# Neighbourhood attention and expert layer on one core: key and query loads in the order of use, the second image's load moved, one mask table

## The chip, the cores and the metric

One core of one Trainium2 chip. The time is the device time of one execution in microseconds (us), all loads and stores included. The engines are TensorE (PE), VectorE (DVE), ScalarE (ACT), GpSimd (POOL) and SyncE (SP). SP computes nothing here: it issues transfers. 16 DMA engines move the data.

## The reference, cut to what matters

Two images of 48 x 48 positions with 384 channels. Twice, the input is group-normalised, goes through a layer and is added to itself. The first layer is attention with 12 heads of width 32, where each position sees a 7 x 7 neighbourhood (moved inwards at the borders) and 16 registers:

```python
qkv = x @ qkv_w.T + qkv_b
scores = jnp.where(mask_cat[None, None], scores * scale, NEG_INF)
attn = jax.nn.softmax(scores, axis=-1)
o = jnp.einsum('bnqk,bnke->bnqe', attn, v_cat)
x = x + (o @ out_w.T + out_b)
```

The second layer is a mixture of four experts of which each position uses the best two. The change doesn't touch it.

## The kernel before, in words

The attention runs in six stages (`gi`, 0 to 5): two images times three groups of four heads. An image is cut in two ways. A *block* `a` (0 to 5) is 8 image rows; a *strip* `s` (0 to 5) is 8 image columns over all 48 rows. Keys are projected by blocks, everything else goes by strips.

A stage goes like this, and all its parts are written out by hand in the order in which each engine runs them; engines meet at semaphores, and each engine, SP and POOL too, goes through its list strictly in order.

1. PE projects the keys of the six blocks. ACT rounds each to fp16 (`KU`), DVE takes the rest (L523) and then copies both halves, opened out into windows, to `KT` (L531); `k_lo` counts the blocks for which both are done. SP writes `KT` to DRAM (`kscr`, L246).
2. PE projects the queries strip by strip (`queries`), between them the output projection of the stage before (`project_out`); POOL writes the queries to DRAM (`qscr`, L358).
3. SP brings keys and queries back in the layout of a strip: `KB` (four slots, three transfers a strip, L254) and `QS` (three transfers a strip, L260). For strips 0, 1, 4 and 5 it first loads 8 mask rows of the slot again (L251), as border strips have other column masks.
4. PE runs the scores that give each query's maximum (`scores`, L1184) in turns with the value projection (`values`). POOL writes the values to DRAM (`vscr`, L365), three transfers a strip, and SP brings them back as windows (`VR`, two buffers, six transfers a strip, L271).
5. PE, ACT and DVE go through the strips: `key_scores` (L1210) gives exponents' inputs, ACT takes the exponential (L890), `weighted` (L1233) sums values and weights. Between them stand the maximum scores of strips 3, 4 and 5. The maxima reach row 120 and 121 of `QS` by POOL's small transfers (L381).

In a stage SP's list is: 12 writes of keys; keys and queries of strips 0, 1, 2, 3; queries of 4 and 5; values of 0 and 1 (which wait until the values of both neighbouring strips have landed in DRAM); then keys of 4 (they wait until strip 0's slot is free), values of 2, keys of 5, values of 3, 4, 5.

The second image is loaded by POOL in stage 0, one sixth (576 KB) in each strip's pass, between its additions of the bias to `X` (L394). Stage 1 reads it first, in the pass of strip 0 (statistics on DVE).

PE waits touched by the change: the query projection of strips 0 and 1 waits for `k_lo` of blocks 2 and 3, since it writes the PSUM banks from which these were read; the first output projection waits for `k_lo` of all six blocks.

Of the kernel before, what the change touches and what calls it, by code (L numbers as in the profile page):

```python
# [17 lines left out]
STRIPS = H // 8  # L18
SN = H * CT_
KW = CT_ + WIN - 1  # L20
X0 = [CT_ * s - 3 for s in range(TILES)]
PADW = W + WIN - 1
CHUNK = P
LEAD, TAIL = 3 * KW + REGS, 3 * KW
# [25 lines left out]
def build(nc, x, wqkv, wo, fc1, fc2, rw, cst, fb2, qtab, ktab, gdown, gup, ident16, tri, pick, out):  # L50
    ctx = ExitStack()
    with ctx:
# [118 lines left out]
        def dve_lows(n, blk):  # L171
# [1 line left out]

        names = """c_in g_in i_in wo_in t_in whi wlo wohi wolo rhi rlo b16 zeros vpad bvhi bvlo bv_mm obx pads ones kr_mm kr_hi kr_lo vr_mm vr_sb krg
            gn_st gn_gs gn_gc gn_mm gn_var gn_sd gn_par gn_hi gn_t gn_ta gn_lo_p gn_lo_v ob_add
            k_mm k_hi k_lo q_mm q_hi q_lo v_mm v_sb o_mm op_done s_mm mx mxh t_mm t_ev st_mm exd pv sumt rinv norm os_hi os_lo
            vreg_in chain f_in fhi flo b2_in b2z b2s moe_in lg_mm ex_in ex_out comb csz ct_mm ct_sb
            h_mm cb_mm ge hf hh hl y_mm y_done y_out""".split()
        s_ = {n: sem(n) for n in names}
# [10 lines left out]
        def kb_count(gi, s):  # L190
            if s in (2, 3):
                return 48 * (gi + 1)
            return 128 * gi + (64 if s < 2 else 128)

        K_BANK = (4, 6, 2, 3, 5, 7)
        V_BANK = lambda gi, s: 7 if gi and s == TILES - 1 else 2 + s % 2
# [32 lines left out]
        def _(sp):  # L229
# [4 lines left out]
            sp.dma_start(raw_g[0], wqkv[:, 0, :]).then_inc(w_in[0], 16)  # L234
            sp.dma_start(QS[96:120, :, :], qtab.unsqueeze(1).broadcast_to([24, HEADS, N])).then_inc(s_["t_in"], 16)
            for i in range(4):
                sp.dma_start(KB[96:TROWS, :, i, :], ktab[1].unsqueeze(1).broadcast_to([26, HEADS, SLOTW])).then_inc(s_["t_in"], 16)
            for g in (1, 2):
                sp.dma_start(raw_g[g], wqkv[:, g, :]).then_inc(w_in[g], 16)
            sp.dma_start(raw_o, wo).then_inc(s_["wo_in"], 16)  # L240
# [5 lines left out]
                    sp.dma_start(kscr[part, :, :, a, :], KT[:, a % 3, part, :, :]).then_inc(kw_out[a % 3], 16)  # L246

            def keys_in(gi, s):
                if s in (0, 1, 4, 5):
                    kind = {0: 0, 1: 1, 4: 1, 5: 2}[s]  # L250
                    sp.dma_start(KB[112:120, :, slot(s), :], ktab[kind, 16:24].unsqueeze(1).broadcast_to([8, HEADS, SLOTW])  # L251
                                 ).then_inc(kb_in[slot(s)], 16)
                for j, part in enumerate((0, 1, 0)):
                    sp.dma_start(KB[DH * j:DH * (j + 1), :, slot(s), LEAD:LEAD + STRIPS * CHUNK],  # L254
                                 kscr[part, :, s, :, :].rearrange("(h d) a n -> d h (a n)", d=DH)).then_inc(kb_in[slot(s)], 16)
# [17 lines left out]
            for gi in range(STAGES):  # L273
                for a in range(STRIPS):
                    keys_out(gi, a)
                for i in range(3):
                    sp.wait_ge(kw_out[i], 64 * gi + 64)
                if gi == 0:
                    sp.wait_ge(s_["t_in"], 16 * 5)
                if 36 * gi > 0:  # L280
                    sp.wait_ge(s_["st_mm"], 36 * gi)
                for s in range(4):
                    keys_in(gi, s)
                    queries_in(gi, s)
                for s in (4, 5):
                    queries_in(gi, s)
                for s in (0, 1):
                    values_in(gi, s)
                for s in range(4):
                    if gi == 4 and s == 2:  # L290
                        for i in (2, 3, 4):
                            sp.wait_ge(v_out[i], 48 * (gi + 1))
                        sp.dma_start(wr_flat, fc1).then_inc(s_["f_in"], 16)
                    if s < 2:
                        sp.wait_ge(s_["st_mm"], 36 * gi + 6 * (s + 1))
                        keys_in(gi, s + 4)
                    values_in(gi, s + 2)
                    if gi == STAGES - 1 and s == 1:
                        for i in (0, 5):
                            sp.wait_ge(v_out[i], 48 * STAGES)  # L300
                        for src, dst in ((fc2, f2raw), (rw, rwraw)):
                            sp.dma_start(dst, src).then_inc(s_["f_in"], 16)
                        for j in range(3):
                            sp.dma_start(b2raw[DH * j:DH * j + EXPERTS, :], fb2).then_inc(s_["b2_in"], 16)
                        sp.dma_start(PICK[0:96, :], pick).then_inc(s_["moe_in"], 16)
# [15 lines left out]
        def _(pool):  # L321
# [75 lines left out]
            for gi in range(STAGES):  # L397
                register_keys(gi)
                for s in range(TILES):
                    queries_out(gi, s)  # L400
                if gi:
                    register_values(gi)
                for s in range(TILES):
                    values_out(gi, s)
                    if gi == 0 and s == 1:
                        register_values(gi)
                    if s in ((3, 4) if gi == 0 else (2, 4)):
                        maxima_in(gi, s // 2 - 1 if gi else s - 3)
                n = {2: 1, 5: 2}.get(gi)
                for s in range(TILES):  # L410
                    for a in range(STRIPS):
                        if a == 1 and s == 0:
                            maxima_in(gi, 2)
                        if a == 5 and s in (1, 2, 3):
                            maxima_in(gi, s + 2)
                        if a == 5 and s:
                            low_output(gi, s - 1)
                        if n and a % 2 == 1:
                            k = a // 2
                            if k in POOL_K[n]:  # L420
                                low_half(n, s, k)
                        if gi in (0, 3) and a % 2 == 0:
                            add_bias(gi // KC, a // 2, s)
                        if gi == 0 and a == 3:
                            c, at = s // 2, s % 2 * 3 * SN
                            pool.dma_start(xs(1, c, at, 3 * SN), x[1, :, c, at:at + 3 * SN]).then_inc(x_in[1][c][s % 2], 16)
                low_output(gi, TILES - 1)

            def hidden_low(m):
# [14 lines left out]
        def _(dve):  # L444
# [75 lines left out]
            def keys_low(gi, a):  # L520
                g = gi % KC
                dve.wait_ge(s_["k_hi"], 6 * gi + a + 1)
                link(V.scalar_tensor_tensor(out=KU[:, a % 2, 1, :, 3:3 + W], in0=ps[:, K_BANK[a], 0:SN].rearrange("p (r c) -> p r c", c=W),  # L523
                                            scalar=cols["qkb16"][:, KC + g:KC + g + 1], in1=KU[:, a % 2, 0, :, 3:3 + W],
                                            op0=ALU.add, op1=ALU.subtract))
                if 64 * gi + 32 * (a // 3) > 0:
                    dve.wait_ge(kw_out[a % 3], 64 * gi + 32 * (a // 3))
                if gi == 0 and a == 0:
                    dve.wait_ge(s_["pads"], 2)
                for part in range(2):  # L530
                    last = V.tensor_copy(KT[:, a % 3, part, :, 0:8 * KW].rearrange("p s (r c) -> p s r c", c=KW), windows(a, part))  # L531
                last.then_inc(s_["k_lo"], 1)
# [531 lines left out]
        def _(pe):  # L1064
# [53 lines left out]

            def queries(gi, s):
                if s < 2:  # L1120
                    pe.wait_ge(s_["k_lo"], 6 * gi + 3 + s)
                else:
                    pe.wait_ge(s_["q_lo"], 6 * gi + s - 1)
                split_product(ps[:, Q_BANK(s), 0:SN], lambda a, k: WQ[:, gi % KC, a, k, 0:P], lambda b, k: xh1(b, k, s * SN, SN)
                              ).then_inc(s_["q_mm"], 1)

            def project_out(gi, s):
                if s == 0:
                    pe.wait_ge(s_["k_lo"], 6 * gi + 12)
                    pe.wait_ge(s_["wolo"], 1)  # L1130
                pe.wait_ge(s_["os_lo"], 6 * gi + s + 1)
                if s == TILES - 1:
# [4 lines left out]
                    if gi in (1, 4):  # L1137
                        pe.wait_ge(s_["gn_par"], (gi + 1) // KC + 2)
                for j in range(KC):
                    if 0 < s < TILES - 1:  # L1140
                        pe.wait_ge(s_["op_done"], 18 * gi + KC * (s - 1) + j + 1)
                    split_product(ps[:, OP_BANK(gi, s, j), 0:SN], lambda a, k: WO[:, a, gi % KC, j * P:(j + 1) * P],
                                  lambda b, k: OS[:, b, s * SN:(s + 1) * SN], steps=1).then_inc(s_["o_mm"], 1)
# [299 lines left out]
def query_table():  # L1443
    import numpy as np
    out = np.zeros((24, TILES, H, CT_), np.float16)
    for r in range(H):
        out[r % 16, :, r, :] = BIG
    for c in range(CT_):
        out[16 + c, :, :, c] = BIG
    return out.reshape(24, N)  # L1450


def key_tables():
    import numpy as np
    out = np.zeros((3, 26, SLOTW), np.float16)
    out[:, 0:24, :] = -BIG
    out[:, 24:26, :] = MSCALE
    first = lambda q, size: min(max(q - WIN // 2, 0), size - WIN)
    for a in range(STRIPS):
        at = LEAD + CHUNK * a  # L1460
        for q in range(max(0, 8 * a - 8), min(H, 8 * a + 16)):
            for r in range(8):
                if first(q, H) <= 8 * a + r < first(q, H) + WIN:
                    out[:, q % 16, at + KW * r:at + KW * (r + 1)] = 0
            if q // 8 == a:
                out[:, q % 16, at + 8 * KW:at + CHUNK] = 0
        for kind, s in enumerate((0, 2, TILES - 1)):
            for c in range(CT_):
                f = first(CT_ * s + c, W)
                for i in range(KW):  # L1470
                    if f <= X0[s] + i < f + WIN:
                        out[kind, 16 + c, at + i:at + 8 * KW:KW] = 0
                out[kind, 16 + c, at + 8 * KW:at + CHUNK] = 0
    return out


# [49 lines left out]
```

## Time and profile before

| | |
|---|---|
| median of 3 runs | 649.22 us (649.11 to 655.11) |
| the profiled execution | 652.61 us, its span 650.8 us |
| PE busy (matmuls) | 567.0 us, 87% of the span |
| DVE, ACT, POOL busy | 455.8, 307.4, 282.7 us |
| DMA packets | 95.44 MB, 147 GB/s over the span |

The profiled execution is 1.81 us longer than its span, and 3.4 us above the median. Busy times are of one engine each and overlap. Stage 0 ends at about 107 us, stage 5 at about 505 us; the rest is the expert layer.

### The profile page before, as it was taken

What the parts mean: (1) busy time and instruction counts of PE and PEld (TensorE: products, weight loads), DVE (VectorE), ACT (ScalarE), POOL (GpSimd) and SP (SyncE); (2) the same over time, 40 slices, a digit from 0 to 9 for tenths busy, and PEclk for the clock granted to TensorE, in tenths of its full rate; (3) what the DMA queues carried; (4) which work ended last, traced back from release to release, by engine and by line L of the source; (5) the groups of instructions that cost most, each with busy time, mean ns of one, the idle gap of its engine ahead of it and who ended that gap; (6) DMA issues with size and microseconds to landing.
All of it is one profiled execution on the core that took longest, in us unless ns stands there. A gap on an engine that the chain in (4) does not pass through costs nothing.

```text
span 650.8 us, 22416 instructions
## 1 busy us (share of the span) xinstructions
PE 567.0 (87%) x9227; PEld 396.7 (61%) x9227; DVE 455.8 (70%) x1021; ACT 307.4 (47%) x609; POOL 282.7 (43%) x421
## 2 busy tenths in 40 slices
PE   3578879998899978998899987897987889998998
PEld 2346666677655756657675766655765546665554
DVE  6885575777887689676667767886689886863333
ACT  1762555215633288513563244541578337754221
POOL 3116798254222654436993362223744332413131
PEclk9999999999999999999999999999989999999999
DMA  9869774995339952398527966189551002121213
GB/s 305 188 148 287 201 217 119 230 275 156 98 89 220 256 144 71 87 255 227 154 57 177 260 177 165 35 201 256 170 145 48 2 0 74 38 74 37 74 37 109
DMA packets 131597, 95.44 MB, mean 147 GB/s; under 512 B 67324, under 2 KB 125352, under 8 KB 131496
## 3 DMA queue, kind: packets, MB, share of 16 engines
q1 hardware_dynamic: 121992, 75.18, 44.8%
q0 software_dynamic: 9504, 18.84, 9.3%
q8 instruction: 73, 1.20, 0.8%
q14 instruction: 28, 0.23, 0.1%
HBM read 57.62 MB, written 35.54 MB: 143 GB/s over the span
## 4 chain that ended last, share of the span: by engine, by line
PE 53%; DVE 16%; DMA 9%; SPq 7%; ACT 6%; issue 6%; POOL 2%; ACTq 0%; POOLq 0%; DVEq 0%
PE ps L1070 38%; SPq L271 5%; PE ps L1233 5%; PE ps L1184 4%; DVE MX L561 3%; DMA vscr<-VT 3%; DMA KB<-kscr 3%; PE ps L1210 3%; DVE ST L454 2%; ACT XH L831 2%; ACT PT L890 1%; DVE GT_ L493 1%; DVE SUMT L574 1%; DVE KT L531 1%; DMA kscr<-KT 1%
## 5 line engine op out<-in xcount | busy, mean ns | idle before, releaser
L561 DVE TENSOR_REDUCE MX<-ps 128x2 f32<-128x372 f32 x216 | 108.3, 541 | 63.9 <-PE ps L1184 62.9
L1070 PE MATMUL ps<-XH,WQ 128*128 128x384 f16 x810 | 140.6, 327 | 8.7 <-DVE XH L503 7.8
L1070 PEld LDWEIGHTS ps<-XH,WQ 128*128 128x128 f16 x810 | 77.6, 98 | 62.6 <-ACT XH L831 7.5
L890 ACT ACTIVATE PT<-ps 128x448 f32<-128x448 f32 (+1 forms) x162 | 78.7, 511 | 52.0 <-PE ps L1210 51.6
L1184 PE MATMUL ps<-KB,QS 120*32 120x186 f16 x1728 | 57.8, 250 | 27.0 <-DVE MX L561 10.6
L434 POOL TENSOR_TENSOR KT<-QS,KT 128x384 f16<-128x384 f32 x36 | 34.3, 962 | 95.3 <-ACT KT L983 95.3
L1210 PE MATMUL ps<-QS,KB 122*128 122x112 f16 (+1 forms) x864 | 64.3, 213 | 12.1 <-ACT PT L890 7.7
L1070 PE MATMUL ps<-WQ,XH 128*128 128x128 f16 x972 | 62.4, 222 | 5.2 <-issue 4.9
L381 POOL DMA_DIRECT2D QS<-MT x72 | 37.8, 529 | 59.5 <-ACT MT L880 59.1
L1210 PEld LDWEIGHTS ps<-QS,KB 122*128 122x128 f16 x864 | 43.3, 99 | 33.1 <-ACT PT L890 16.6
L1070 PEld LDWEIGHTS ps<-WQ,XH 128*128 128x128 f16 x972 | 56.0, 99 | 11.2 <-issue 8.8
L1233 PE MATMUL ps<-PT,VR 128*32 128x112 f32 (+1 forms) x1296 | 60.1, 258 | 2.5 <-DMA VR<-vscr 2.5
L1233 PE MATMUL ps<-PT,ONE 128*32 128x112 f32 (+1 forms) x1296 | 59.5, 254 | 0.8 <-issue 0.8
L1070 PE MATMUL ps<-OS,WO 128*128 128x384 f16 x324 | 57.6, 326 | 2.5 <-DVE X L545 1.5
L1070 PE MATMUL ps<-KT,WQ 128*128 128x384 f16 x324 | 58.6, 326 | 0.8 <-DVE X L726 0.5
L1184 PEld LDWEIGHTS ps<-KB,QS 120*32 120x32 f16 x1728 | 31.5, 97 | 43.5 <-DVE MX L561 16.8
L386 POOL TENSOR_TENSOR OS<-ON,OS 128x384 f16<-128x384 f32 x36 | 33.2, 922 | 33.2 <-ACT OS L896 32.9
L719 DVE TENSOR_TENSOR QS<-ps,QS 128x384 f32<-128x384 f32 x36 | 19.7, 555 | 39.1 <-POOL KT L434 14.1
L1070 PEld LDWEIGHTS ps<-OS,WO 128*128 128x128 f16 x324 | 31.0, 98 | 25.0 <-issue 3.0
L1070 PEld LDWEIGHTS ps<-KT,WQ 128*128 128x128 f16 x324 | 30.9, 98 | 23.8 <-DVE X L726 3.4
L394 POOL TENSOR_SCALAR X<-X,SM 128x384 f32<-128x384 f32 x36 | 44.4, 1242 | 0.4
L358 POOL DMA_DIRECT2D qscr<-QT x18 | 13.3, 741 | 71.2 <-DVE QT L537 71.1
(168 smaller groups left out, 1003.3 us busy)
## 6 DMA issues: line engine op xcount, KB each, us to landing
KB<-kscr SPq DMA_DIRECT2D x108, 192.0 KB, 7.0
kscr<-KT SPq DMA_DIRECT2D x72, 192.0 KB, 2.5
VR<-vscr SPq DMA_DIRECT2D x216, 56.0 KB
QS<-qscr SPq DMA_DIRECT2D x108, 96.0 KB, 6.6
out<-X SPq DMA_DIRECT2D x11, 576.0 KB, 3.3
X<-in_x SPq DMA_DIRECT2D x6, 576.0 KB, 7.3
qscr<-QT POOLq DMA_DIRECT2D x18, 192.0 KB, 3.3
qscr<-PT POOLq DMA_DIRECT2D x18, 192.0 KB, 5.3
```

Of the source, the lines that this page charges most:

```text
L271: sp.dma_start(VR[0:8 * KW, s % 2, a, :], vscr[8 * a:8 * a + 8, CT_ * s:CT_ * s + KW, :]).then_inc(vr_in[s % 2][a // 3], 16)
L381: pool.dma_start(QS[SROWS + part:SROWS + part + 1, :, s * SN:(s + 1) * SN], MT[part * HEADS:(part + 1) * HEADS, s % 2, :]).then_inc(m_in[s ...
L386: nc.gpsimd.tensor_tensor(OS[:, 1, s * SN:(s + 1) * SN], ON[:, s % 2, :], OS[:, 0, s * SN:(s + 1) * SN], ALU.subtract).then_inc(s_["os_lo" ...
L394: nc.gpsimd.tensor_scalar(xs(img, c, s * SN, SN), xs(img, c, s * SN, SN), cols["obx"][:, c:c + 1], None, ALU.add).then_inc(s_["ob_add"], 1)
L434: nc.gpsimd.tensor_tensor(HW[:, m % 2, 1, k, :], HF[:, unit % 2, :], HW[:, m % 2, 0, k, :], ALU.subtract).then_inc(s_["hl"], 1)
L561: V.tensor_reduce(out=MX[:, s % 2, t, 2 * pair:2 * pair + 2], in_=ps[:, S_BANK(s, i), 0:2 * RUN].rearrange("p (h n) -> p h n", h=2), op=AL ...
L719: V.tensor_tensor(HF[:, unit % 2, :], ps[:, 2 + k, 0:SN], GE[:, unit % 2, :], ALU.mult).then_inc(s_["hf"], 1)
L890: A(PTS[n % 4][:, 0:w], ps[:, ST_BANK(n), 0:w], ACT.Exp, scale=SCORE).then_inc(s_["exd"], 1)
L1070: last = mm(bank, lhsT(a, k), rhs(b, k), start=(k == 0 and n == 0), stop=(finish and k == steps - 1 and n == 2))
L1184: last = mm(ps[32 * j:32 * j + 32, S_BANK(s, i), hh * RUN:(hh + 1) * RUN], QS[0:SROWS, h, q0:q0 + 32], KB[0:SROWS, h, slot(s), at:at + RUN ...
L1210: last = mm(ps[:, ST_BANK(n), h * w:(h + 1) * w], KB[0:TROWS, h, slot(s), LEAD + CHUNK * a:LEAD + CHUNK * (a + 1)], QS[0:TROWS, h, s * SN ...
L1233: last = mm(ps[DH * h:DH * (h + 1), bank, CT_ * q0:CT_ * q1], lhsT, PTS[n % 4][:, h * w:(h + 1) * w], start=(a == 0), stop=(a == STRIPS - ...
```

## The change

- SP loads keys and queries of strips 0, 1 and 2, then waits until the six score units of strip 0 are done (`s_mm`), loads strip 3's keys and queries, then values of strips 0 and 1, and only then the queries of strips 4 and 5.
- The mask of all strips comes from one key table; the border strips' difference is put in the query table. The four mask loads of a stage go.
- The second image's six loads go from the six strip passes of stage 0 to the last three, two in each.
- A new semaphore `k_ps` counts the blocks whose PSUM bank DVE has read (L523), before the copies to `KT`. The query projections of strips 0 and 1 wait for it, and the first output projection waits bank by bank (blocks 1, 4, 5 of the next stage) in place of `k_lo`.

```diff
             def keys_in(gi, s):
-                if s in (0, 1, 4, 5):
-                    kind = {0: 0, 1: 1, 4: 1, 5: 2}[s]
-                    sp.dma_start(KB[112:120, :, slot(s), :], ktab[kind, 16:24].unsqueeze(1).broadcast_to([8, HEADS, SLOTW])
-                                 ).then_inc(kb_in[slot(s)], 16)
                 for j, part in enumerate((0, 1, 0)):
...
-                for s in range(4):
+                for s in range(3):
                     keys_in(gi, s)
                     queries_in(gi, s)
+                sp.wait_ge(s_["s_mm"], 36 * gi + 6)
+                keys_in(gi, 3)
+                queries_in(gi, 3)
+                for s in (0, 1):
+                    values_in(gi, s)
                 for s in (4, 5):
                     queries_in(gi, s)
-                for s in (0, 1):
-                    values_in(gi, s)
...
-                        if gi == 0 and a == 3:
-                            c, at = s // 2, s % 2 * 3 * SN
-                            pool.dma_start(xs(1, c, at, 3 * SN), x[1, :, c, at:at + 3 * SN]).then_inc(x_in[1][c][s % 2], 16)
+                        if gi == 0 and s > 2 and a in (1, 4):
+                            c, half = s - 3, a // 4
+                            at = half * 3 * SN
+                            pool.dma_start(xs(1, c, at, 3 * SN), x[1, :, c, at:at + 3 * SN]).then_inc(x_in[1][c][half], 16)
...
-                link(V.scalar_tensor_tensor(out=KU[:, a % 2, 1, :, 3:3 + W], in0=ps[:, K_BANK[a], 0:SN].rearrange("p (r c) -> p r c", c=W),
+                V.scalar_tensor_tensor(out=KU[:, a % 2, 1, :, 3:3 + W], in0=ps[:, K_BANK[a], 0:SN].rearrange("p (r c) -> p r c", c=W),
...
+                                       op0=ALU.add, op1=ALU.subtract).then_inc(s_["k_ps"], 1)
+                dve.wait_ge(s_["k_ps"], 6 * gi + a + 1)
...
                 if s < 2:
-                    pe.wait_ge(s_["k_lo"], 6 * gi + 3 + s)
+                    pe.wait_ge(s_["k_ps"], 6 * gi + 3 + s)
...
                 if s == 0:
-                    pe.wait_ge(s_["k_lo"], 6 * gi + 12)
...
-                    if 0 < s < TILES - 1:
+                    if s == 0:
+                        pe.wait_ge(s_["k_ps"], 6 * gi + (8, 11, 12)[j])
+                    elif s < TILES - 1:
```

## Rows read from the trace of the kernel before

**Rows 1.** Whom PE waited for, whole span: us in total, times, longest

```profile
PE ps L1184 <- issue: 6.9, 6, 3.4
PE ps L1184 <- DMA KB<-kscr: 6.7, 6, 1.7
PE ps L1070 <- issue: 4.9, 4, 1.9
...
PE ps L1233 <- DMA VR<-vscr: 3.1, 4, 1.6
...
PE ps L1070 <- DVE KT L531: 1.0, 2, 0.7
```

**Rows 2.** Timeline of SP in stage 4: start, us, issues merged by line

```profile
366.73 1.59 SPq L254 DMA_DIRECT2D KB<-kscr  x3
368.37 4.71 SPq L260 DMA_DIRECT2D QS<-qscr  x9
379.95 8.41 SPq L271 DMA_DIRECT2D VR<-vscr  x12
388.40 0.49 SPq L251 DMA_DIRECT2D KB<-in_ktab  x1
388.93 2.15 SPq L254 DMA_DIRECT2D KB<-kscr  x3
391.20 4.13 SPq L271 DMA_DIRECT2D VR<-vscr  x6
...
395.90 1.26 SPq L254 DMA_DIRECT2D KB<-kscr  x3
```

**Rows 3.** The chain of waits in stage 4: start, us, what

```profile
372.80 1.18 POOL vscr L365 x3
...
374.36 5.53 DMA vscr<-VT
...
390.65 3.17 DMA KB<-kscr
...
396.73 4.25 DMA KB<-kscr
```

**Rows 4.** DMA queues from 371 to 376 us: packets, MB, share of 16 engines

```profile
q1 hardware_dynamic: 1196, 1.10, 104.4%
q0 software_dynamic: 24, 0.03, 2.9%
```

**Rows 5.** Busy time by stretch, stage 4; last three: PEclk, DMA share, GB/s

```profile
380.00:384.00 4.00, 3.00 (x59) 2.26 (x58) 3.07 (x9) 2.51 (x7) 4.00 (x9) 1.00 0.44 126
```

**Rows 6.** Timeline of PE in stage 4: start, us, work [idle before it, until whom]

```profile
368.72 0.66 PE L1184 MATMUL ps<-KB,QS 120*32 120x186 f16 x24
...
393.86 0.50 PE L1184 MATMUL ps<-KB,QS 120*32 120x186 f16 x16 [1.65 <-DMA KB<-kscr]
...
401.03 0.50 PE L1184 MATMUL ps<-KB,QS 120*32 120x186 f16 x16 [1.15 <-DMA KB<-kscr]
```

**Rows 7.** Timeline of PE in stage 5

```profile
454.71 0.81 PE L1184 MATMUL ps<-KB,QS 120*32 120x186 f16 x15 [3.43 <-issue]
```

**Rows 8.** Busy time by stretch, stage 5 and stage 0

```profile
454.00:458.00 4.00, 3.29 (x41) 3.00 (x41) 1.00 (x2) 0.00 (x0) 0.00 (x0) 0.57 1.06 305
60.00:64.00 4.00, 2.14 (x49) 1.88 (x53) 1.04 (x3) 0.84 (x2) 2.19 (x5) 0.74 1.09 297
```

**Rows 9.** POOL's loads of the second image (duration ns), and their landing

```profile
L426 POOL DMA_DIRECT2D X<-in_x x6: 583/615/617, 77.0 to 106.1; - x6
...
DMA to landing us min/median/max: 4.4/4.6/5.1
```

**Rows 10.** The chain of waits in stage 0

```profile
83.59 5.40 DMA QS<-MT
```

**Rows 11.** Timeline of PE in stage 0

```profile
83.03 0.50 PE L1184 MATMUL ps<-KB,QS 120*32 120x186 f16 x16 [1.33 <-DMA KB<-kscr]
...
89.12 0.51 PE L1210 MATMUL ps<-QS,KB 122*128 122x88 f16 x8 [0.52 <-DMA QS<-MT]
```

More of the change, by code:

```diff
@@ L20 @@
 KW = CT_ + WIN - 1
-X0 = [CT_ * s - 3 for s in range(TILES)]
 PADW = W + WIN - 1
@@ L175, in build @@
             gn_st gn_gs gn_gc gn_mm gn_var gn_sd gn_par gn_hi gn_t gn_ta gn_lo_p gn_lo_v ob_add
-            k_mm k_hi k_lo q_mm q_hi q_lo v_mm v_sb o_mm op_done s_mm mx mxh t_mm t_ev st_mm exd pv sumt rinv norm os_hi os_lo
+            k_mm k_hi k_ps k_lo q_mm q_hi q_lo v_mm v_sb o_mm op_done s_mm mx mxh t_mm t_ev st_mm exd pv sumt rinv norm os_hi os_lo
             vreg_in chain f_in fhi flo b2_in b2z b2s moe_in lg_mm ex_in ex_out comb csz ct_mm ct_sb
@@ L192, in kb_count @@
                 return 48 * (gi + 1)
-            return 128 * gi + (64 if s < 2 else 128)
+            return 96 * gi + (48 if s < 2 else 96)
         K_BANK = (4, 6, 2, 3, 5, 7)
@@ L236, in _ @@
             for i in range(4):
-                sp.dma_start(KB[96:TROWS, :, i, :], ktab[1].unsqueeze(1).broadcast_to([26, HEADS, SLOTW])).then_inc(s_["t_in"], 16)
+                sp.dma_start(KB[96:TROWS, :, i, :], ktab.unsqueeze(1).broadcast_to([26, HEADS, SLOTW])).then_inc(s_["t_in"], 16)
             for g in (1, 2):
@@ L522, in keys_low @@
                 dve.wait_ge(s_["k_hi"], 6 * gi + a + 1)
-                link(V.scalar_tensor_tensor(out=KU[:, a % 2, 1, :, 3:3 + W], in0=ps[:, K_BANK[a], 0:SN].rearrange("p (r c) -> p r c", c=W),
-                                            scalar=cols["qkb16"][:, KC + g:KC + g + 1], in1=KU[:, a % 2, 0, :, 3:3 + W],
-                                            op0=ALU.add, op1=ALU.subtract))
+                V.scalar_tensor_tensor(out=KU[:, a % 2, 1, :, 3:3 + W], in0=ps[:, K_BANK[a], 0:SN].rearrange("p (r c) -> p r c", c=W),
+                                       scalar=cols["qkb16"][:, KC + g:KC + g + 1], in1=KU[:, a % 2, 0, :, 3:3 + W],
+                                       op0=ALU.add, op1=ALU.subtract).then_inc(s_["k_ps"], 1)
+                dve.wait_ge(s_["k_ps"], 6 * gi + a + 1)
                 if 64 * gi + 32 * (a // 3) > 0:
@@ L1448, in query_table, with key_table @@
     for c in range(CT_):
-        out[16 + c, :, :, c] = BIG
+        out[16 + max(c, 3), 0, :, c] = BIG
+        out[16 + c, 1:TILES - 1, :, c] = BIG
+        out[16 + min(c, 4), TILES - 1, :, c] = BIG
     return out.reshape(24, N)
-def key_tables():
+def key_table():
     import numpy as np
-    out = np.zeros((3, 26, SLOTW), np.float16)
-    out[:, 0:24, :] = -BIG
-    out[:, 24:26, :] = MSCALE
+    out = np.zeros((26, SLOTW), np.float16)
+    out[0:24, :] = -BIG
+    out[24:26, :] = MSCALE
     first = lambda q, size: min(max(q - WIN // 2, 0), size - WIN)
@@ L1463, in key_tables @@
                 if first(q, H) <= 8 * a + r < first(q, H) + WIN:
-                    out[:, q % 16, at + KW * r:at + KW * (r + 1)] = 0
+                    out[q % 16, at + KW * r:at + KW * (r + 1)] = 0
             if q // 8 == a:
[L1466 to L1473, printed above, removed]
+                out[q % 16, at + 8 * KW:at + CHUNK] = 0
+        for c in range(CT_):
+            for i in range(c, c + WIN):
+                out[16 + c, at + i:at + 8 * KW:KW] = 0
+            out[16 + c, at + 8 * KW:at + CHUNK] = 0
     return out
@@ L1513 @@
         "rw": flat(np.asarray(L1_conv_router_w).T),
-        "cst": np.ascontiguousarray(np.concatenate(consts, axis=1)), "fb2": np.ascontiguousarray(L1_conv_fc2_b), "qtab": query_table(), "ktab": key_tables(),
+        "cst": np.ascontiguousarray(np.concatenate(consts, axis=1)), "fb2": np.ascontiguousarray(L1_conv_fc2_b), "qtab": query_table(), "ktab": key_table(),
         "gdown": rows(member / np.float32(C // GROUPS)), "gup": np.ascontiguousarray(member.T), "ident16": np.eye(P, dtype=np.float16),
```

## The prediction, made before the change was timed

> **What bounds the kernel now.** I read the waits of PE over the whole span first, then one stage in detail: SP's timeline, the chain of waits, the DMA queues and PE's timeline, all of stage 4, and last the places in stages 0 and 5 that differ. The expert layer, 505 us to the end, is not touched and drops out.
>
> The change can only win back PE time that lies idle in the attention. [rows 1] shows what there is. Six waits for keys loaded to `KB` cost 6.7 us, four waits for `VR` 3.1 us, two waits for DVE's copies to `KT` 1.0 us. Ten waits have the releaser "issue": 6.9 + 4.9 = 11.8 us in which no semaphore was awaited. I read these as PE's sequencer waiting for its own instructions, since they fall into stretches where the DMA engines are full and break off in the middle of a unit of matmuls that all wait for the same thing. That reading is an inference; no row names the fetch.
>
> In stage 4 the order of things is this. SP issues keys of strip 3 at 366.73 and nine query transfers up to 373.08 [rows 2]. POOL issues the values' writes of strips 0 and 1 until 373.98, and the last of them lands at 374.36 + 5.53 = 379.89 [rows 3]. Only then can SP start the values' loads, at 379.95, and from there it is busy without a gap: 8.41 us for twelve loads, 0.49 for a mask, 2.15 for keys of strip 4, 4.13 for six more loads, 0.48 for a mask, 1.26 for keys of strip 5 [rows 2]. The two sets of keys land at 390.65 + 3.17 = 393.82 and 396.73 + 4.25 = 400.98 [rows 3], and PE starts the scores of strips 4 and 5 at 393.86 and 401.03, having waited 1.65 and 1.15 us [rows 6]. So in this stage PE's time is set by SP's list behind the landing of the values. Stages 1 and 3 have the same pattern: with stage 0's 1.33 us [rows 11] and these 2.80 taken from the 6.7, they hold the other 2.6 us. What PE loses in those stages before strip 4 is given back at that wait, so a shorter stall there gains nothing unless the keys also come earlier.
>
> **The change part by part, stages 1, 3 and 4.** The new order puts six query issues between the values of strips 0 and 1 and the keys of strip 4. Nine such issues took 4.71 us [rows 2], so six take 3.1. The mask ahead of the keys goes, 0.49. Keys of strip 4 would be issued 2.6 us later if the values landed when they do now; keys of strip 5, with a second mask gone, 2.1 us later. Queued behind the same six issues on SP are the values of strips 2 to 5; they follow the keys and have no wait in stage 4.
>
> Against that stands an earlier start. From 371 to 376 us SP's queue (q1) filled the DMA engines to 104.4% and moved 1.10 MB, while POOL's queue (q0), to which the values had been handed from 371.75 on, got 2.9% [rows 4]. The values stood behind what SP had already handed over. The queries of strips 4 and 5 are 6 x 96 KB = 0.59 MB of that; at the 0.22 MB/us of this stretch they are worth 2.7 us. SP's new wait holds strip 3 back until the second score group of strip 0, which ends at 368.72 + 0.66 = 369.4 [rows 6], 2.7 us later than its issue now. With 1.59 + 1.6 us of issue strip 3 is handed over by 372.6, still ahead of nearly all of the values. That wait alone hides behind the values' projection; strip 3 isn't needed before the passes begin, at about 381 us. If it came late, PE would stall at the first scores of strip 3. So I take the values 2.7 us earlier. With a landing as short as 3.17 us [rows 3] the last write would come at 373.98 + 3.17 = 377.15, also 2.7 earlier. The bounds: 0, if the queries do not stand in their way, and 3.4, which would need a landing in 2.5 us, shorter than any in these rows. Then keys of strip 4 come at 2.6 - 2.7 = about 0, keys of strip 5 at -0.6. The queries now share the DMA engines with the keys, but those are at a share of 0.44 there [rows 5]. The `VR` waits of stage 4 vanish, and are absorbed by the keys' wait. Result: stage 4 -0.5, stage 3, where only the keys of strip 4 bind, 0. Stage 1 would be -0.5 like stage 4, but starts later (below): 0. Bounds for the three together: +2.1 + 2.6 + 2.1 = +6.8 with values unmoved, -3.4 - 0.5 + 2.6 = -1.3 each, so -3.9 in all, with values at their earliest.
>
> The Trainium skill, page "DMA: Bandwidth & Descriptors", section "Queues, rings and completion order", says that each DMA engine takes turns between the queues that have work, a packet from each. By that rule the values would never have waited for all of SP's queue, and taking queries out of it would help little: the sum would be nearer +6.8 than 0. The 104.4% against 2.9% [rows 4] speaks against turns in this stretch, for work that one queue had got in first; part of the delay can still be POOL's own time from issue to the first packet.
>
> **`k_ps`.** DVE reads each bank before it copies twice, so the PE waits end earlier by two copies, some 0.6 us a block. What PE now loses to these copies is 1.0 us in two waits, the longest 0.7 [rows 1]; they stand at the first output projection in stages 4 and 5. They go: -1.0. In stage 4 this shifts PE, and with it the values and SP's list, so it counts there too. DVE's own order and its wait after L523 stay as they are: 0.
>
> **The masks.** 24 loads of 54 KB go. Two of four in a stage are on SP's path and are counted; the first two lie in SP's slack: 0. The tables' work on host data costs nothing on the device.
>
> **Stage 0.** Here SP is not behind: it waits for PE before the keys of strip 4. Those take long to land because a load of the second image is under way (each takes 4.4 to 5.1 us [rows 9]); with none in the first three passes, and no mask, the 1.33 us wait [rows 11] goes. The maxima of strip 3 took 5.40 us to land, behind such a load [rows 10], and PE lost 0.5 us to that [rows 11]; gone too. In return the load at `a == 4` of strip 3's pass now stands directly ahead of the maxima of strip 5 in POOL's list and queue. If they take the same 5.40 us, PE, which comes to the last pass some 3 to 5 us after their issue, waits for them; I put 0.6 us, between 0 and 2.4. Two loads a pass also meet the values of strip 5, whose wait of 1.6 us (among the four of [rows 1]) may grow by up to 2. Sum for stage 0: -1.33 - 0.5 + 0.6 = -1.2, bounds -3.4 (its `VR` wait gone too) and +2.4. POOL pays 0.6 us for each of three more issues in the last passes [rows 9], so it starts stage 1's register copies some 1 to 1.8 us later, and with them SP's writes of keys; the last image load is in flight there. This takes stage 1's 0.5 us and no more, as PE projects for 20 us before its first scores.
>
> **Waits on "issue".** Less traffic ahead of the values also means less ahead of a fetch. In stages 1, 3 and 4 the keys absorb it. In stage 2 two waits of about 0.7 us are left; I count half, -0.7. In stage 5 one wait took 3.43 us [rows 7], and behind it PE's granted clock fell to its lower level (1.2 GHz): 0.57 on average over 4 us, worth 0.43 x 4 = 1.7 us [rows 8]. Nothing downstream absorbs it, as keys of strip 4 land well ahead. Whether it shrinks depends on what is in the queue at that moment: SP's pause between strip 2 and strip 3 falls just before. Half: -2.5, bounds 0 and -5.1.
>
> **The sum.** -0.5 (stage 4) - 1.0 (`k_ps`) - 1.2 (stage 0) - 0.7 (stage 2) - 2.5 (stage 5) = -5.9, so 652.61 - 5.9 = 646.7 for the profiled execution. That one is 3.4 us above the median, which is just the size of the long wait in stage 5; if the usual execution doesn't have it, the change earns 3.4 without it, and 649.22 - 3.4 = 645.8. I take 646.0.
>
> **Rivals.** (a) The order costs more than it gives: the values land when they do now, because what they wait for is the keys and not the queries. Then six query issues push the keys of strips 4 and 5 back: +6.8, with -3.4 from the other terms, +3.4: 652.6. It decides from a gain at the values' landing below about 1.5 us. For it: SP's list is gapless there [rows 2] and the rule of turns above, of which it is the mechanism in this kernel. Against it: [rows 4]. (b) The stalls on "issue" go altogether, in stage 0 (1.7 us and 1.7 of clock: 0.26 x 4 plus as much again behind it [rows 8]), 2 and 5: 0.7 and 2.5 more and 3.4 for stage 0, and values come at their earliest: -3.4: 649.22 - 3.4 - 0.7 - 3.4 - 3.4 = 638.3. For it: 11.8 us are there [rows 1]. Against it: traffic is only moved by some us, and ahead of the fetches it is the same. (c) The change does not do what it says: the wait for `s_mm` ends when SP would have got there anyhow and loads land as before, or the gains are absorbed stage by stage: 649.
>
> **How the numbers follow.** Forecast 0.55 (642 to 650), rival (a) 0.15 (650 to 657), (b) 0.18 (636 to 642), (c) 0.12. About 1%, 6.5 us, is what a measurement of this kernel can tell from no change. Faster than 642.7: nearly all of (b) and a sixth of the forecast, 0.27. Slower than 655.7: a fifth of (a), and stage 0's upper bound on top of others, 0.08. Same: 0.65. The range, 638 to 653, leaves out half of (b) and a quarter of (a).
>
> **What would show it.** In stage 4 the chain should have the values' last write landing about 2.7 us after its issue less than now, SP's loads from about 377.3 (relative to the same first scores), six query issues behind them, and the keys of strip 4 issued near 388.7; PE's wait for them should be 1.5 to 3 us, having taken over what other waits lose. PE's waits on `KT` should be gone, and stage 0's wait for `KB`, with one for `QS<-MT` before the last pass in its place. The prediction is wrong if the values' writes land after 379 as now, if PE waits over 3.5 us for the keys of strip 4, or if the waits on "issue" shrink by more than half.

## The result, and the profile after

The changed kernel takes 655.22 us (median of 19 runs), the kernel before 653.2 us in 19 runs beside it: ratio 1.0045, 95% interval 1.0023 to 1.0067. It is slower, by 0.45%, where 646.0 us and a gain were forecast. The profiled execution took 654.1 us, its span 652.3. The 649.22 us that the prediction started from was the median of three runs; with nineteen it is 653.2, so the profiled execution of before, 652.61 us, was an ordinary one. Of the 9.2 us between the 646.0 us forecast and the 655.22 us measured, 4.0 us lie in that starting value and 5.2 us in the change: -3.2 us forecast, +2.0 us measured.

The waits of PE over the whole span are the first thing to read, against [rows 1] (the list gives us in total, times, longest).

```profile
PE ps L1185 <- DMA KB<-kscr: 20.3, 6, 4.7
...
PE ps L1070 <- issue: 2.5, 2, 1.4
...
PE ps L1211 <- DMA QS<-MT: 1.8, 1, 1.8
...
PE ps L1234 <- DMA VR<-vscr: 1.1, 3, 0.8
```

The waits on "issue" fell from 11.8 to 2.5 us, those on `VR` from 3.1 to 1.1, those on `KT` are gone. That is 12.3 us won. The waits for keys grew from 6.7 to 20.3 us, 13.6 us lost, and the wait for the maxima (`QS<-MT`) from 0.5 to 1.8 us, 1.3 us lost. PE's timeline shows where: one long wait in each of the stages 1 to 5, for strip 4, and none for strip 5.

```profile
160.55 0.81 PE L1185 MATMUL ps<-KB,QS 120*32 120x186 f16 x16 [4.71 <-DMA KB<-kscr]
...
241.49 0.65 PE L1185 MATMUL ps<-KB,QS 120*32 120x186 f16 x16 [3.12 <-DMA KB<-kscr]
...
321.29 0.81 PE L1185 MATMUL ps<-KB,QS 120*32 120x186 f16 x16 [4.34 <-DMA KB<-kscr]
...
398.08 0.81 PE L1185 MATMUL ps<-KB,QS 120*32 120x186 f16 x16 [4.71 <-DMA KB<-kscr]
...
479.28 0.50 PE L1185 MATMUL ps<-KB,QS 120*32 120x186 f16 x16 [2.90 <-DMA KB<-kscr]
```

SP's timeline in stage 4, beside [rows 2], and PE's first scores of that stage:

```profile
372.80 1.25 SPq L249 DMA_DIRECT2D KB<-kscr  x3
374.10 2.54 SPq L255 DMA_DIRECT2D QS<-qscr  x3
381.13 8.77 SPq L266 DMA_DIRECT2D VR<-vscr  x12
389.95 3.11 SPq L255 DMA_DIRECT2D QS<-qscr  x6
393.11 1.38 SPq L249 DMA_DIRECT2D KB<-kscr  x3
394.61 4.14 SPq L266 DMA_DIRECT2D VR<-vscr  x6
398.79 2.32 SPq L249 DMA_DIRECT2D KB<-kscr  x3
```

```profile
369.88 0.67 PE L1185 MATMUL ps<-KB,QS 120*32 120x186 f16 x24
```

All times of a stage are best counted from its first scores, at 369.88 here and at 366.51 before (one group of three score units and one value projection, 2.2 us, ahead of the 368.72 of [rows 6]). SP starts the values' loads at 11.2 us instead of 13.4, 2.2 earlier. It issues the keys of strip 4 at 23.2 us instead of 22.4, as the six query issues (3.11 us) stand ahead of them. The keys have landed and PE goes on at 28.2 us instead of 27.4. But PE was there at 23.5 us, where before it came at 25.7: what it had won by then it lost at this wait, and 0.8 us more.

The chain of waits in the same stretch, beside [rows 3]. The last write of the values lands after 3.34 us instead of 5.53, the keys of strip 4 after 3.98 instead of 3.17.

```profile
377.74 3.34 DMA vscr<-VT
...
394.05 3.98 DMA KB<-kscr
```

The DMA queues from 374.37 to 379.37 us (packets, MB, share of 16 engines). Like [rows 4] this stretch begins 4.5 us behind the first scores, 0.7 us ahead of POOL's first issue of values. POOL's queue gets a quarter of the engines, where it had 2.9%.

```profile
q1 hardware_dynamic: 881, 0.88, 77.9%
q0 software_dynamic: 191, 0.38, 24.9%
```

At each long wait the granted clock fell to 1.2 GHz, half of full speed. Busy time in such a stretch of stage 4 (last three columns: PEclk, DMA share, GB/s):

```profile
396.00:400.00 4.00, 1.92 (x48) 1.89 (x52) 1.00 (x3) 0.00 (x0) 0.00 (x0) 0.50 0.53 129
```

By the ends of the last sums (L1233 before, L1234 after) the six stages took 106.5, 75.3, 83.3, 74.5, 76.9 and 88.8 us before, and 104.4, 79.5, 83.7, 75.9, 77.2 and 86.2 after. Stage 0 and stage 5 won 2.1 and 2.6 us; stage 1 lost 4.2, stages 2, 3 and 4 together 2.1. The expert layer is the same in both.

### The profile page after: what moved, and what is told of

Its sections match the earlier page's. It is cut to its first block, busy times and chain, and to the rows that moved or that the text cites. A ratio compares the mean times of both kernels' runs of the same rounds, so it can differ in the third digit from the quotient of the medians.

```text
span 652.3 us, 22392 instructions
## 1 busy us (share of the span) xinstructions
PE 571.9 (88%) x9227; PEld 402.5 (62%) x9227; DVE 452.5 (69%) x1021; ACT 307.1 (47%) x609; POOL 282.4 (43%) x421
## 4 chain that ended last, share of the span: by engine, by line
PE 61%; DVE 14%; DMA 9%; SPq 6%; ACT 5%; issue 4%; POOL 1%; ACTq 0%; DVEq 0%; POOLq 0%
PE ps L1070 40%; PE ps L1234 7%; PE ps L1185 5%; PE ps L1211 4%; DMA KB<-kscr 4%; SPq L266 4%; DVE MX L561 3%; DVE ST L453 2%; DMA vscr<-VT 2%; ACT PT L890 1%; DMA VR<-vscr 1%; ACT XH L831 1%; DVE GT_ L492 1%; DMA X<-in_x 1%; SPq L255 1%
## 5 line engine op out<-in xcount | busy, mean ns | idle before, releaser
L1185 PE MATMUL ps<-KB,QS 120*32 120x186 f16 x1728 | 59.2, 258 | 28.7 <-DMA KB<-kscr 20.3
L1211 PE MATMUL ps<-QS,KB 122*128 122x112 f16 (+1 forms) x864 | 66.0, 217 | 12.9 <-ACT PT L890 7.3
L1211 PEld LDWEIGHTS ps<-QS,KB 122*128 122x128 f16 x864 | 44.9, 101 | 34.7 <-ACT PT L890 16.0
L1234 PE MATMUL ps<-PT,VR 128*32 128x112 f32 (+1 forms) x1296 | 62.2, 267 | 1.1 <-DMA VR<-vscr 1.1
L1070 PE MATMUL ps<-WQ,XH 128*128 128x128 f16 x972 | 60.5, 220 | 2.9 <-issue 2.5
L1234 PE MATMUL ps<-PT,ONE 128*32 128x112 f32 (+1 forms) x1296 | 60.7, 262 | 0.0
L1070 PEld LDWEIGHTS ps<-WQ,XH 128*128 128x128 f16 x972 | 54.4, 98 | 8.2 <-issue 5.5
```

What stands on the lines that cost most here:

```text
L1070: last = mm(bank, lhsT(a, k), rhs(b, k), start=(k == 0 and n == 0), stop=(finish and k == steps - 1 and n == 2))
L1185: last = mm(ps[32 * j:32 * j + 32, S_BANK(s, i), hh * RUN:(hh + 1) * RUN], QS[0:SROWS, h, q0:q0 + 32], KB[0:SROWS, h, slot(s), at:at + RUN ...
L1211: last = mm(ps[:, ST_BANK(n), h * w:(h + 1) * w], KB[0:TROWS, h, slot(s), LEAD + CHUNK * a:LEAD + CHUNK * (a + 1)], QS[0:TROWS, h, s * SN ...
L1234: last = mm(ps[DH * h:DH * (h + 1), bank, CT_ * q0:CT_ * q1], lhsT, PTS[n % 4][:, h * w:(h + 1) * w], start=(a == 0), stop=(a == STRIPS - ...
```

## The experiments

All ratios are to the kernel before, measured beside it on the same chip. Traces are of one execution each. The first four, and the shorter wait, ask what SP's order does; then come the clock, the parts one by one, and the best order again.

**The order alone.** The kernel before, with SP's new list and nothing else.

```diff
-                for s in range(4):
+                for s in range(3):
                     keys_in(gi, s)
                     queries_in(gi, s)
+                sp.wait_ge(s_["s_mm"], 36 * gi + 6)
+                keys_in(gi, 3)
+                queries_in(gi, 3)
+                for s in (0, 1):
+                    values_in(gi, s)
                 for s in (4, 5):
                     queries_in(gi, s)
-                for s in (0, 1):
-                    values_in(gi, s)
```

> The kernel before with nothing but SP's new order and its wait for the first scores; masks, image loads and the waits for k_lo as before. Theory 1 (the order alone makes it slower): KB waits of 3 to 5 us in stages 1 to 5, granted clock at half behind them, ratio 1.008 to 1.015. Rival (another part, such as the later image load, costs): ratio 1.000 or below, KB waits under 10 us in sum.

Measured: 666.14 us, ratio 1.0194 (1.0144 to 1.0243), at the upper end of what was expected or above it. PE's waits for keys:

```profile
PE ps L1187 <- DMA KB<-kscr: 28.3, 7, 5.6
```

The order alone makes the kernel before slower by 1.9%.

**Everything but the order.** The changed kernel with the old list.

```diff
-                for s in range(3):
+                for s in range(4):
                     keys_in(gi, s)
                     queries_in(gi, s)
-                sp.wait_ge(s_["s_mm"], 36 * gi + 6)
-                keys_in(gi, 3)
-                queries_in(gi, 3)
-                for s in (0, 1):
-                    values_in(gi, s)
                 for s in (4, 5):
                     queries_in(gi, s)
+                for s in (0, 1):
+                    values_in(gi, s)
```

> The changed kernel with SP's old order and without its wait: one mask table, the image loads in the last three passes and k_ps stay. Theory 1: ratio 0.992 to 0.996, as stage 0 saves 1.2 to 2.2 us, k_ps 1.0 and the masks on SP's path about 1.5 in three stages; the waits on issue are back at 8 us or more. Rival (the image load moved to the end of stage 0 costs more in stage 1 than it saves): ratio 1.000 to 1.004.

Measured: 645.73 us, 0.9886 (0.9840 to 0.9933). The rest of the change is a gain of 1.1%, more than the 0.4 to 0.8% expected, though the interval reaches into that. The order turns it into a loss of 0.45%. PE's waits here: the keys cost little, "issue" is back.

```profile
PE ps L1182 <- issue: 5.9, 5, 1.9
PE ps L1182 <- DMA KB<-kscr: 4.8, 6, 1.3
PE ps L1067 <- issue: 3.7, 4, 1.8
```

**The queries of strips 4 and 5 ahead of the values.** The changed kernel, with one move in SP's list; the wait for the scores stays.

```diff
                 queries_in(gi, 3)
-                for s in (0, 1):
-                    values_in(gi, s)
                 for s in (4, 5):
                     queries_in(gi, s)
+                for s in (0, 1):
+                    values_in(gi, s)
```

> The changed kernel, but with the queries of strips 4 and 5 issued right behind strip 3 and ahead of the values of strips 0 and 1; SP's wait for the first scores stays. Theory 1 (six query issues between values and keys of strip 4 are the loss; queries and values share one backlog): values land up to 2.7 us later, keys of strip 4 come 3.1 us of issue earlier and without queries beside them; PE's waits for KB fall from 20.3 us to about 12, and the ratio to the kernel before is about 0.998. Rival (DMA engines take turns, values do not move): the KB waits nearly vanish and the ratio is 0.985 to 0.990. Rival (the order is not the cause): ratio stays 1.003 to 1.006.

Measured: 642.3 us, 0.9829 (0.9782 to 0.9876). This one move is worth 2.2% against the changed kernel. Of what was expected, the rival came nearest: the values do not land later. Its reason, that the DMA engines take turns, does not follow from that. SP's timeline in stage 4, whose first scores are at 364.27:

```profile
368.49 5.12 SPq L255 DMA_DIRECT2D QS<-qscr  x9
375.65 9.40 SPq L266 DMA_DIRECT2D VR<-vscr  x12
385.09 1.40 SPq L249 DMA_DIRECT2D KB<-kscr  x3
```

The values' loads start at 11.4 us behind the first scores, as in the changed kernel (11.2), although six more query loads were issued in the meantime; the keys of strip 4 are issued at 20.8 us instead of 23.2. The queries go out while SP would wait for the values' landing anyway: in the changed kernel it stood idle there for 3.6 to 6.3 us in stages 1 to 5. The pause for the first scores also puts them behind the values on their way to the DMA engines. POOL issues the values' writes of strips 0 and 1 from 3.1 to 6.9 us behind the first scores (in stage 4 from 5.2 to 8.4), and SP the six query loads from 6.4 us on or later. PE's waits for keys are at 5.8 us:

```profile
PE ps L1185 <- DMA KB<-kscr: 5.8, 5, 1.8
```

**Without the wait for the first scores.** The changed kernel, less one line.

```diff
-                sp.wait_ge(s_["s_mm"], 36 * gi + 6)
```

> The changed kernel without SP's wait for the first scores: strip 3 is loaded at once, then values of strips 0 and 1, then queries of 4 and 5. Theory 1 (the wait is what brings the values in earlier, the queries' place is what loses): values land 12.5 us or more behind the first scores instead of 11.2, KB waits above 20 us in sum, ratio to the kernel before 1.008 to 1.014. Rival (the queries' place behind the values is what brings them in earlier, the wait is idle): as the changed kernel or better, 1.001 to 1.005.

Measured: 653.56 us, 1.0018 (0.9997 to 1.0039), KB waits of 14.8 us in sum. The expectation that the wait brings the values in early fell: their loads started at 9.4 to 11.2 us without it. With this run the four orders form a table; columns three and four are means over stages 1 to 5, in us behind the first scores, read from SP's timelines of one execution each. The first four rows are the changed kernel but for SP's list; the last has the masks, the old place of the image loads and `k_lo` as well.

```
queries 4, 5        wait   values' loads start   keys of strip 4 issued   ratio
ahead of values     no     12.1                  20.7                     0.9886 (0.9840 to 0.9933)
ahead of values     yes    11.3                  20.7                     0.9829 (0.9782 to 0.9876)
behind values       no     10.5                  22.9                     1.0018 (0.9997 to 1.0039)
behind values       yes    11.2                  23.1                     1.0045 (1.0023 to 1.0067)
(the kernel before) no     12.4                  21.9                     1
```

Over the first four rows the ratio follows the fourth column and not the third. Queries behind the values make these start 1.5 us earlier without the wait, nothing with it, and delay the keys by 2.2 and 2.4 us on balance. The wait itself: the intervals of the first two rows overlap, and so do those of the third and fourth. Its effect on the time is not shown.

**A shorter wait.** The run with the queries ahead, waiting for three score units instead of six.

```diff
-                sp.wait_ge(s_["s_mm"], 36 * gi + 6)
+                sp.wait_ge(s_["s_mm"], 36 * gi + 3)
```

> The run with the queries of strips 4 and 5 ahead of the values, with SP's wait shortened to the first three score units of strip 0 (2.2 us earlier). Theory 4 (the pause lets POOL's values in ahead of strip 3 and the late queries, and is worth 0.6%): with a shorter pause values land later than 11.3 us behind the first scores, ratio 0.985 to 0.990. Rival (the pause is worth nothing): 0.983, as with the longer one.

Measured: 643.77 us, 0.9883 (0.9832 to 0.9933). The values start at 11.9 to 12.5 us, as expected for a shorter pause; the interval doesn't tell the ratio from that of either neighbour. The six query loads are now issued from 3.4 us on, beside the values' writes or ahead of them, and the values' loads start as late as without a pause: at 12.2 us on average, against 12.1 without a pause and 11.3 with the full one. POOL's queue in stage 4 shows the same. The rows are of the stretch from 4.5 to 9.5 us behind the first scores, beside [rows 4]; first with the short pause:

```profile
q0 software_dynamic: 48, 0.11, 7.5%
```

With the full pause:

```profile
q0 software_dynamic: 145, 0.31, 18.8%
```

Without a pause (everything but the order):

```profile
q0 software_dynamic: 51, 0.10, 6.9%
```

So in these runs the values come later where the query loads are handed over ahead of their writes or beside them. The masks alone, below, do not fit in.

**Is it the clock?** The changed kernel, with PE kept at work ahead of the wait.

```diff
                 if i == 0:
+                    if s == 4 and DUMMY:
+                        pe.wait_ge(s_["mx"], 36 * gi + 23)
+                        for _ in range(DUMMY):
+                            mm(ps[:, S_BANK(s, i), 0:SN], WO[:, 0, 0, 0:P], WO[:, 0, 1, 0:C], start=True, stop=True)
                     pe.wait_ge(kb_in[slot(s)], kb_count(gi, s))
```

> The changed kernel with 24 extra matmuls of 384 columns (about 3.9 us) on PE in each stage ahead of its wait for the keys of strip 4, so that PE works while it would wait; results are overwritten. Theory 2 (a part of the loss is the clock: behind each long wait the granted clock stays at half for 3.4 or 6.8 us): no half-clock stretch in stages 1, 3 and 4, about 2 us saved in each, but up to 3.9 us lost in stage 0, and about 1 in stages 2 and 5, where PE waited less: ratio to the kernel before 0.999 to 1.003. Rival (PE is not what limits these stretches): nothing saved, ratio 1.010 to 1.014.

Measured: 661.52 us, 1.0137 (1.0084 to 1.0189), as the rival had it. In stage 4 the extra matmuls took the place of the wait, and the clock stayed at 2.4 GHz:

```profile
398.77 4.07 PE L1165 MATMUL ps<-WO 128*128 128x384 f16 x24
```

```profile
404.00:408.00 4.00, 3.56 (x128) 2.89 (x117) 3.83 (x11) 1.81 (x4) 0.00 (x0) 1.00 0.64 177
```

Stage 1 was 2.4 us shorter than in the changed kernel, stage 4 equal (77.1 against 77.2), stages 2, 3 and 5 longer by 0.5, 0.8 and 1.8; stage 0 lost 5.6 us, where PE had hardly waited. In sum over stages 1 to 5 nothing was saved (403.1 against 402.6 us), although the granted clock stood at 1.2 GHz for 31 us of these stages in the changed kernel and for 3.4 us here. That the fallen clock is a part of the loss is not borne out in the sum. It isn't refuted either: in stages 2 and 5 the extra matmuls (4.07 us in stage 4) took longer than the wait that they filled (3.12 and 2.90 us), and the run can't tell this price from what the clock may have given back.

**The masks alone.** The kernel before with one key table, the border strips' difference in the query table, and no mask loads.

```diff
...
             def keys_in(gi, s):
-                if s in (0, 1, 4, 5):
-                    kind = {0: 0, 1: 1, 4: 1, 5: 2}[s]
-                    sp.dma_start(KB[112:120, :, slot(s), :], ktab[kind, 16:24].unsqueeze(1).broadcast_to([8, HEADS, SLOTW])
-                                 ).then_inc(kb_in[slot(s)], 16)
...
```

> The kernel before with one mask table and without the 24 mask loads. Theory: about 0.5 us less on SP's path ahead of strip 4's keys and of strip 5's in stages 1, 3 and 4, 1.5 to 3 us in all, ratio 0.995 to 0.998. Rival (the mask loads also hold up what stands behind them in the DMA engines, so their removal is worth more): 0.990 to 0.994, and it is most of what the changed kernel with the old order gained.

Measured: 647.25 us, 0.9924 (0.9894 to 0.9953): 5.0 us, two thirds of what everything but the order gives, and in the rival's range. In stage 4, whose first scores are at 366.47, it looks like this (SP's timeline; then DMA queues from 371 to 376 us, beside [rows 4]):

```profile
377.42 8.76 SPq L267 DMA_DIRECT2D VR<-vscr  x12
386.23 1.40 SPq L250 DMA_DIRECT2D KB<-kscr  x3
```

```profile
q1 hardware_dynamic: 1380, 1.01, 86.7%
q0 software_dynamic: 157, 0.34, 20.6%
```

The values' loads start 11.0 us behind the first scores instead of 13.4, as early as with the new order; POOL's queue got 20.6% of the engines in this stretch where it had 2.9%. Over stages 1 to 5 the start moved from 12.4 to 11.2 us, the keys' issue from 21.9 to 20.1. That is 1.2 us of earlier landing on top of the 0.5 us of the issue itself. But the run with everything but the order has no masks either, and the same list on SP, and there the values start at 12.1 us on average, with 6.9% for POOL's queue in that stretch. What is measured is the 0.8% of the time; that the missing masks bring the values in earlier is not shown.

**Half of the masks.** Two runs leave out the mask loads of two strips each, so that a border strip uses another strip's mask.

```diff
...
-                if s in (0, 1, 4, 5):
+                if s in (4, 5):
```

> The kernel before, with the mask loads of strips 0 and 1 left out (strip 0 then uses the mask of another strip, so its border columns see wrong neighbours); those of strips 4 and 5 stay. Theory 3 (the masks ahead of the keys slow the backlog in which the values wait, as the run with one mask table showed values landing 10.9 us instead of 13.4 behind the first scores): values land 10.9 to 11.9 us behind the first scores, ratio 0.993 to 0.996. Rival (only SP's issues ahead of strips 4 and 5 count, as the prediction had it): ratio 0.999 to 1.000.

```diff
...
-                if s in (0, 1, 4, 5):
+                if s in (0, 1):
```

> The kernel before, with the mask loads of strips 4 and 5 left out (strip 5 then uses another strip's mask); those of strips 0 and 1 stay. Theory 3: values land as before, 13 us or more behind the first scores, 0.5 us of SP's path saved twice in a stage: ratio 0.997 to 0.999. Rival: the whole gain of 0.8% is here, ratio 0.991 to 0.994.

Measured: 651.68 us, 0.9975 (0.9935 to 1.0016) without the masks of strips 0 and 1, and 651.56 us, 0.9997 (0.9971 to 1.0023) without those of 4 and 5. Neither is told from no change. The second interval leaves out 0.991 to 0.994, so the whole gain does not sit with strips 4 and 5. The values' loads start 11.5 us behind the first scores on average without the masks of strips 0 and 1 and 12.2 us without those of 4 and 5 (12.4 before, 11.2 with no mask loads): the direction of theory 3, but smaller than the difference between the two runs without any mask loads, 0.9 us. Where the 0.8% sit is not settled.

**`k_ps` alone**, with this as its core:

```diff
...
-                    pe.wait_ge(s_["k_lo"], 6 * gi + 3 + s)
+                    pe.wait_ge(s_["k_ps"], 6 * gi + 3 + s)
...
```

> The kernel before with k_ps and the waits on it alone. Prediction's theory: two waits of 1.0 us in sum go, ratio 0.998 to 0.999. Rival (the waits stand in front of longer ones and are taken up there): 1.000.

Measured: 651.2 us, 0.9981 (0.9947 to 1.0014). As expected in size, not told from nothing.

**The image loads alone.**

```diff
-                        if gi == 0 and a == 3:
+                        if gi == 0 and s > 2 and a in (1, 4):
...
```

> The kernel before with the second image's loads in the last three passes of stage 0. Theory: stage 0 loses its 1.3 us wait for KB and gains one of 1.5 to 2.2 us for the maxima of strip 5, stage 1 starts its keys later by 1 us: ratio 0.999 to 1.002. Rival (the old place cost more than its two waits show): 0.996 or less.

Measured: 649.07 us, 0.9970 (0.9935 to 1.0006), not told from nothing either. The expected trade of waits in stage 0 is not in its trace: a `KB` wait of 1.24 us remains, now ahead of strip 5, and no wait on `QS<-MT` is there.

**The best order with the image loads in their old place.**

```diff
-                        if gi == 0 and s > 2 and a in (1, 4):
+                        if gi == 0 and a == 3:
...
```

> The run with the queries of strips 4 and 5 ahead of the values, with the image loads back in all six passes of stage 0. Theory: the late place costs a wait for the maxima of strip 5 of about 2 us and 1 us at the start of stage 1, but saves 1.3 us of a KB wait: ratio 0.982 to 0.985, within 0.3% of the run with the late place. Rival (the image's place is worth 0.3% as the run with it alone had it): 0.985 to 0.988.

Measured: 641.42 us, 0.9849 (0.9801 to 0.9897). Within the interval of the 0.9829 with the late place: these runs show no effect of the image's place, and can't tell one of some tenths of a per cent. Both versions beat the kernel before and the changed one.

## Why the prediction was wrong

- **What bounds a stage** was read rightly: PE's losses ahead of strip 4 come back at the wait for its keys, and only earlier keys help. In stages 1, 3 and 4 this is what happened, and in 2 and 5 as well.
- **The step that failed** is "so I take the values 2.7 us earlier", set against 2.6 us of added issues, from which the keys of strip 4 were to come at about 0. In the changed kernel the values' loads start 1.2 us earlier on average over stages 1 to 5 (12.4 to 11.2), 2.2 us in stage 4, while the six query issues push the keys back by 2.8 to 4.1 us; the keys of strip 4 are issued 1.2 us later than before (21.9 to 23.1). The queries' place alone is worth 1.5 us of earlier values without the pause (12.1 to 10.5) and nothing with it (11.3 to 11.2). The argument was made from stage 4 alone, where the values landed latest of all stages (13.4 us, elsewhere 12.0 to 12.2), so where most was to be won.
- **Whom the values waited for.** I took [rows 4] as proof that the values stand behind whatever SP had handed over. The four orders and the shorter pause bear this out in kind and not in size: with query loads ahead of the values' writes or beside them the values' loads start at 12.1 and 12.2 us, with none there at 10.5 to 11.3. The Trainium skill, page "DMA: Bandwidth & Descriptors", section "Queues, rings and completion order", says that a DMA engine takes turns between its queues, a packet from each. By that rule the queries' place would have moved the values little. No run shows such turns: POOL's queue got 2.9, 6.9 and 7.5% in stage 4 where the queries came first, and 18.8 and 24.9% where they came later. The 20.6% of the run with the masks alone, where the queries came first too, is against this reading and stays unexplained, and how much of a small share is POOL's own time up to its first packet was not measured.
- **Rival (a)** had the right place and sign: six query issues ahead of the keys of strip 4. It got 0.15. Its condition, that the values gain less than about 1.5 us, was met on average (1.2) and not in stage 4 (2.2), and its premise, values landing as now, was not. It put the keys 2.6 us later in a stage, where 1.2 us were measured against the kernel before; its sum of +3.4 us is near the +2.0 of the medians, but by another account: the new order costs 1.6% in the changed kernel (0.9886 to 1.0045), and the rest gave back 1.1%.
- **"Nothing downstream absorbs it, as keys of strip 4 land well ahead"**, said for stage 5 and assumed for stage 2, was false: the waits for these keys there are 3.12 and 2.90 us. The waits on "issue" did fall, by 9.3 of 11.8 us, more than the half forecast, but PE reached the same late keys earlier. Stage 5 won 2.6 us, as forecast for its long wait; stage 2 nothing.
- **The masks** were mis-sized: "the first two lie in SP's slack: 0", and 0.5 us of issue for each of the others. Measured alone they are worth 5.0 us; why is open.
- **Stage 0** and the last maxima: forecast -1.2 us, measured -2.1 for the stage; the new wait for `QS<-MT` came, with 1.8 us instead of 0.6, and the `KB` wait of 1.33 us for strip 4 went, with one of 0.54 us for strip 5 in its place. POOL's lateness was said to cost stage 1 at most 0.5; the stage reached its first scores 28.3 us after its start instead of 27.3. There the chain shows a write of keys that took 4.73 us to land, and then PE waits 0.83 us behind DVE's pass over the queries:

```profile
113.41 4.73 DMA kscr<-KT
```

- **The clock** behind a longer wait was left out of rival (a). It fell in five stages, yet its cost could not be shown.
- **The signs of being wrong** that the prediction named: PE waited 4.71 us for the keys of strip 4, over the 3.5, and the waits on "issue" shrank by more than half. The third did not come: the values' writes landed 2.2 us earlier in stage 4.
- **Rival (b)** lists 2.5 us more in stage 5, which its sum of 638.3 doesn't contain.

## What to carry to other kernels

Before a transfer's issue is moved in a queue's list, look at what the queue does at either place: here SP waited 3.6 to 6.3 us for the values anyway, so the issues were nearly free ahead of them and cost 2.8 to 4.1 us behind. Look also at what stands beside it on the DMA engines: in most runs here a queue's writes landed later when another queue's loads had been handed over ahead of them. A stall that vanishes upstream is no gain until the thing that ends last downstream comes earlier too; count every stage from a common event, and put the arrival of the consumer beside the arrival of its data. A term that is a difference of two guesses of the same size (2.6 less 2.7) deserves the width of both, and a look at every stage, not at the one with the largest number.

## What was not expected of the hardware

Removing 24 loads of 54 KB, 1.3 of 95.4 MB, took 0.8% off the time. The two half removals could not place the gain, and what in these loads costs so much is open.

The waits on "issue" can be read more closely than the prediction did. In the kernel before there are twelve in the attention, the two of L1233 included, and ahead of every one of them a block of 16 KB on DMA queue 8, which the profile calls "instruction", has ended 1.2 to 1.7 us before PE goes on; so it is with all ten of the run with everything but the order. There are 73 such blocks in 650.8 us, too few for this to be chance. It supports the reading that PE waited for its instructions. The block ahead of the longest wait (3.43 us, to 454.71) is in the DMA queues from 451.5 to 453.2 us:

```profile
q8 instruction: 1, 0.02, 4.9%
```
